# Reading index columns in place, with a memset ahead of each indirect transfer, in a graph network kernel

## What is computed

```python
h = relu(layernorm(x)); x = x + spmm(spmm(h))                 # L0: two weighted hops
h = relu(layernorm(x)); x = x + gcn(h, W, b)                   # L1: normalised by degree, one product
h = relu(layernorm(x)); x = x + (relu((h + sum_src h) @ W1.T + b1) @ W2.T + b2)        # L2
h = relu(layernorm(x)); x = x + update([h, sum_e message([h[src], h[dst], edge_attr])])  # L3: two small networks
```

## Time and profile before

| | us |
|---|---|
| median of 3 runs | 4911.03 |
| lowest, highest | 4899.02, 4911.47 |
| the profiled execution's own time | 4916.42 |
| its span, first to last instruction | 4914.2 |

### The profile page before, as it was taken

How to read it: one execution, slowest core, us unless ns; L and a number is a source line. 1 busy time by engine, 2 the same in 40 slices (tenths; PEclk the granted TensorE clock), 3 DMA queues, 4 the chain that set the end, 5 groups by cost and what they waited for, 6 DMA issues and landing times.

```text
span 4914.2 us, 62117 instructions
## 1 busy us (share of the span) xinstructions
PE 3612.6 (74%) x18706; PEld 2888.8 (59%) x18706; DVE 3039.2 (62%) x7232; ACT 2012.8 (41%) x5132; POOL 3807.9 (77%) x4405
## 2 busy tenths in 40 slices
PE   4767666666499999957777778878458787778784
PEld 2444344444399989945555556666346665656663
DVE  5634444444456566658888858888557666566661
ACT  3434434434311111135555555656225454454452
POOL 6788888888778888877788558888677888888875
PEclk8667767766655555578898989999779898998896
DMA  8433333332344454433343324444333223232220
GB/s 285 100 56 45 56 56 45 57 56 28 50 91 86 83 92 84 55 71 123 104 133 104 117 78 156 153 149 164 131 99 111 67 84 100 71 112 68 71 69 20
DMA packets 335499, 452.19 MB, mean 92 GB/s; under 512 B 208111, under 2 KB 233301, under 8 KB 334740
## 3 DMA queue, kind: packets, MB, share of 16 engines
q1 hardware_dynamic: 159268, 361.69, 20.9%
q0 software_dynamic: 176000, 87.72, 15.5%
HBM read 258.41 MB, written 225.53 MB: 98 GB/s over the span
## 4 chain that ended last, share of the span: by engine, by line
POOL 38%; issue 14%; PE 10%; DVE 6%; DMA 2%; ACT 2%; DVEq 0%; SPq 0%; POOLq 0%; ACTq 0%; another core or an unknown queue 0%
POOL ga L929 19%; POOL out_x L1062 8%; POOL isl L925 5%; POOL xu L1002 3%; PE tp L1259 2%; PE tp L1246 2%; POOL osl L925 2%; PE mm L1104 2%; PE mm L1123 1%; DMA xu<-acc,osl 1%; DVE xf L1948 1%; DVE wide L2107 1%; PE mm L1135 1%; PE mm L1097 1%; ACT zx L1597 1%
## 5 line engine op out<-in xcount | busy, mean ns | idle before, releaser
L929 POOL DMA_INDIRECT ga<-table,isl x784 | 838.8, 1070 | 224.4 <-issue 113.7
L1002 POOL DMA_INDIRECT xu<-acc,osl x392 | 625.1, 1595 | 144.8 <-issue 106.2
L1209 PE MATMUL tp<-xw,cc 128*128 128x394 f32 x784 | 411.5, 623 | 334.7 <-DVE cc L2015 243.3
L929 POOL DMA_INDIRECT ga<-xu,isl x392 | 424.1, 1082 | 111.8 <-POOL isl L925 61.5
L1062 POOL DMA_INDIRECT out_x<-acc,osl x392 | 418.6, 1068 | 114.5 <-POOL osl L925 80.8
L1209 PEld LDWEIGHTS tp<-xw,cc 128*128 128x128 f32 x784 | 141.3, 220 | 592.6 <-issue 324.9
L1246 PE MATMUL tp<-us,wide 128*128 128x64 f32 x1568 | 416.9, 422 | 88.9 <-DVE us L2143 50.0
L1246 PEld LDWEIGHTS tp<-us,wide 128*128 128x128 f32 x1568 | 379.9, 332 | 93.7 <-DVE us L2143 50.2
L1259 PE MATMUL tp<-acc,wide 128*128 128x64 f32 x1560 | 423.1, 427 | 0.8
L1194 PE MATMUL tp<-us,wide 128*128 128x64 f32 x1568 | 343.9, 421 | 69.6 <-DVE us L1932 60.8
L1562 ACT ACTIVATE acc<-tp,h 128x64 f32<-128x64 f32 x392 | 101.7, 310 | 693.2 <-PE tp L1259 541.9
(11 more groups left out here) (377 smaller groups left out, 9733.1 us busy)
## 6 DMA issues: line engine op xcount, KB each, us to landing
wide<-xu SPq DMA_DIRECT2D x84, 448.0 KB
zx<-key_rows SPq DMA_DIRECT2D x28, 896.0 KB
out_x<-wide SPq DMA_DIRECT2D x56, 448.0 KB
table<-acc SPq DMA_DIRECT2D x56, 448.0 KB
xf<-xs SPq DMA_DIRECT2D x56, 448.0 KB
wide<-table SPq DMA_DIRECT2D x56, 448.0 KB
xu<-in_x SPq DMA_DIRECT2D x25, 1000.0 KB
hop_even<-zeros SPq DMA_DIRECT2D x1, 12544.0 KB
```

Source lines behind the costliest of these rows:

```text
L929: nc.gpsimd.indirect_dma_start(o[:, g, :], None, table, bass.IndirectOffsetOnAxis(idx[:, g:g + 1], 0)).then_inc(s, 16)
L1002: nc.gpsimd.indirect_dma_start(xu, bass.IndirectOffsetOnAxis(osl[b][:, g:g + 1], 0), acc[b][:, g, :], None, compute_op=ALU.add).then_inc(f ...
L1209: f.key_row.raise_by(nc.tensor.matmul(tp[1][:, at:at + KEYS], reach[:, g * P:g * P + P], key_steps, start=True, stop=True), ("g", b, g))
```

## The change

POOL no longer copies index columns. The transfer is given the column of the big index tile itself. Ahead of each such transfer POOL now writes zeros to a tile `spacer` of 128 x 128 floats that nobody reads. The transfer does not wait for this memset; the next memset waits for the one before it. In `t_scatter` the wait for earlier scatters goes, since no slot is overwritten. All of it concerns the 56 gathers ahead of the first hop, the 392 + 392 gathers of the sparse stages, and the 784 transfers of the last stage: 1,624 in all. `hop0` and `hop1` stay as they are.

```diff
+        spacer = sb("spacer", [P, P])
...
-            def slot_copy(o, i_):
-
-                return nc.gpsimd.tensor_copy(o, i_).then_inc(s_slot, 1)
-
...
-            def gather_by_column(o, table, slot, index, c, s, copied):
+            def gather_spaced(o, table, index, c, s, spaced):
 
                 for g in range(G):
-                    slot_copy(slot[:, g:g + 1], index[:, c + g:c + g + 1])
-                    after.wait_ge(s_slot, copied + g + 1)
-                    gather(o, table, slot, s, (g,))
-                return copied + G
+                    if spaced + g:
+                        after.wait_ge(s_slot, spaced + g)
+                    nc.gpsimd.memset(spacer[:, :], 0.0).then_inc(s_slot, 1)
+                    gather(o, table, index[:, c:c + G], s, (g,))
+                return spaced + G
...
             for u in range(4):
-                copied = gather_by_column(ga_of[u], x, isl_of[u], dstc_i, u * G, f.got[u], copied)
+                spaced = gather_spaced(ga_of[u], x, dstc_i, u * G, f.got[u], spaced)
...
-                        copied = gather_by_column(ga[b], table, isl[b], index, ecol(i, b), f.got[b], copied)
-                    return copied
+                        spaced = gather_spaced(ga[b], table, index, ecol(i, b), f.got[b], spaced)
+                    return spaced
...
-            def t_scatter(i, copied, first=False):
+            def t_scatter(i, spaced):
                 for b in B2K:
                     after.wait_ge(*tt.o_ready.at(i, ("o", b)))
-                    if not first:
-
-                        after.wait_ge(tt.written[b], 16 * G * i)
                     for g in range(G):
-                        slot_copy(osl[b][:, g:g + 1], out_idx[:, tcol(i, b) + g:tcol(i, b) + g + 1])
-                        after.wait_ge(s_slot, copied + b * G + g + 1)
+                        after.wait_ge(s_slot, spaced + b * G + g)
+                        nc.gpsimd.memset(spacer[:, :], 0.0).then_inc(s_slot, 1)
                         nc.gpsimd.indirect_dma_start(
-                            out, bass.IndirectOffsetOnAxis(osl[b][:, g:g + 1], 0), acc[b][:, g, :], None,
+                            out, bass.IndirectOffsetOnAxis(out_idx[:, tcol(i, b) + g:tcol(i, b) + g + 1], 0),
+                            acc[b][:, g, :], None,
                             bounds_check=nodes_max, oob_is_err=False).then_inc(tt.written[b], 16)
-                return copied + 2 * G
+                return spaced + 2 * G
```

More of the change, by code:

```diff
@@ L380, in gnn @@
         s_answer = sem("prep_products_in_psum")
-        s_slot = sem("pool_slot_copied")
+        s_slot = sem("pool_spacer_written")
         s_turned = sem("keys_turned")
@@ L930, in gather @@
                         o[:, g, :], None, table, bass.IndirectOffsetOnAxis(idx[:, g:g + 1], 0)).then_inc(s, 16)
-            def gather_by_column(o, table, slot, index, c, s, copied):
+            def gather_spaced(o, table, index, c, s, spaced):
                 for g in range(G):
-                    slot_copy(slot[:, g:g + 1], index[:, c + g:c + g + 1])
-                    after.wait_ge(s_slot, copied + g + 1)
-                    gather(o, table, slot, s, (g,))
-                return copied + G
+                    if spaced + g:
[3 more added lines that the diff above has]
+                return spaced + G
             after.wait_ge(s_node, 1)
-            copied = 0
+            spaced = 0
             hop_max, all_max = pool.to_reg(ROWS + 4 * P - 1), pool.to_reg(ROWS + N + 4 * P - 1)
@@ L1019, in _, with body @@
                         after.wait_ge(sp_[0].kept[b], 2 * 16 * STEPS)
-                def body(i, first, copied):
+                def body(i, first, spaced):
                     for b in B2K if k == 0 else B2K[::-1]:
@@ L1028, in body @@
                                 after.wait_ge(*f.ga_free.at(i - 1, ("g", b)))
-                        copied = gather_by_column(ga[b], table, isl[b], index, ecol(i, b), f.got[b], copied)
-                    return copied
+                        spaced = gather_spaced(ga[b], table, index, ecol(i, b), f.got[b], spaced)
+                    return spaced
                 for i in range(STEPS):
-                    copied = body(i, i == 0, copied)
+                    spaced = body(i, i == 0, spaced)
                 for b in B2K:
@@ L1043, in _, with t_gather @@
                 after.wait_ge(s_fixed, 32 * (k + 1))
-            def t_gather(i, copied, first=False):
+            def t_gather(i, spaced, first=False):
                 for b in B2K:
@@ L1049, in t_gather @@
                         after.wait_ge(*tt.ga_free.at(i - 1, ("g", b)))
-                    copied = gather_by_column(ga[b], tables[1], isl[b], ptr_i, tcol(i, b), tt.got_a[b], copied)
-                return copied
-            def t_scatter(i, copied, first=False):
+                    spaced = gather_spaced(ga[b], tables[1], ptr_i, tcol(i, b), tt.got_a[b], spaced)
+                return spaced
+            def t_scatter(i, spaced):
                 for b in B2K:
                     after.wait_ge(*tt.o_ready.at(i, ("o", b)))
-                    if not first:
-                        after.wait_ge(tt.written[b], 16 * G * i)
@@ L1064, in t_scatter @@
                             bounds_check=nodes_max, oob_is_err=False).then_inc(tt.written[b], 16)
-                return copied + 2 * G
+                return spaced + 2 * G
             for q in LANES:
                 after.wait_ge(s_dense[q], 16 * DSTEPS)
[L1069 to L1073, removed]
+            spaced = t_gather(0, spaced, True)
@@ L1074, in _ @@
+            spaced = t_gather(1, spaced)
+            spaced = t_gather(2, spaced)
+            spaced = t_scatter(0, spaced)
+            spaced = t_gather(3, spaced)
             for i in range(2, STEPS - 2):
-                copied = t_scatter(i - 1, copied)
-                copied = t_gather(i + 2, copied)
+                spaced = t_scatter(i - 1, spaced)
+                spaced = t_gather(i + 2, spaced)
             for i in (STEPS - 3, STEPS - 2):
-                copied = t_scatter(i, copied)
+                spaced = t_scatter(i, spaced)
@@ L1083, in _ @@
                                          bounds_check=rows_max, oob_is_err=False).then_inc(s_head, 16)
-            t_scatter(STEPS - 1, copied)
+            t_scatter(STEPS - 1, spaced)
             after.wait_ge(s_border, 5)
```

## The result

The changed kernel takes 4707.15 us (median of 4 runs, 4706.33 to 4711.23), the kernel before 4907.63 us beside it: a ratio of 0.9595, with a 95% interval of 0.9579 to 0.9612. That is 4.05% or 200 us less. The forecast was 4726 us.

What follows compares the result with a forecast made beforehand. POOL, busy 77% of the span, was taken as the bound, with some 1263 transfers on the chain. Gaps 152 us plus stalls 53 less 20 given back left 185, so 4726 us; range 4630 to 4870.

Steps and rivals of the forecast that it cites:

- new gap 0.35 us, a gain of 0.12: POOL between indirect transfers: gap 0.01 + 0.14 + 0.20 = 0.35 us against 0.47; 1263 x 0.12 = 152 us.
- The memset's hold: Ahead of each transfer: 128 columns hold POOL 0.14 us, by a straight line between memsets of one and 448 columns.
- The stalls: POOL's copies beside VectorE instructions reading two full tiles: 107 us of stalls on the chain, half of them, 53 us, gained.
- What is given back: First sparse stage and last stage: 20 us taken off because VectorE and TensorE are close to binding.
- The larger gain: Rival, chance 0.20: transfer's start runs beside the memset, gap 0.30 us, no memset stalls; 282 us gained, 4629 us.
- My slower rival: Rival, chance 0.12: the 0.27 us ahead of a transfer is its own and stays; between 4927 and 4980 us.
- the smaller gain: Rival, chance 0.18: memset counts with 0.20 us and stalls like copies, or TensorE and VectorE bind at once; 4842 us.
- no effect: Rival, chance 0.05: waits for tiles take up the shorter round, or memset and stall cancel the gain; 4911 us.

## Why the prediction was right, point by point

The mechanism was right: the wait and the copies' stalls are what the change takes away, and both parts are seen by themselves. That the number is off by 19 us only is in part luck, since three terms were off and their errors nearly cancel.

**The wait.** Step "new gap 0.35 us, a gain of 0.12": measured 0.38 and 0.09, and 0.02 more from a gather that takes 0.95 instead of 0.97, which I hadn't foreseen. Idle ahead of a transfer came out at 0.16 to 0.17 us where I had 0.14. From start to start an undisturbed round of a gather fell by 0.108 us and that of a scatter by 0.084. Over the 1263 transfers on the chain (392 of them scatters) that makes an estimate of 127 us where the sum has 152. The 139 us of the run with the wait put back are another difference: the kernel with the waited memset has a gap of 0.49 us and not 0.47, since its memset is longer than the copy.

**The memset's hold.** A straight line through the memsets of the earlier trace rows was right in slope between 96 and 256 columns: the recorded medians are 0.192, 0.205, 0.219 and 0.327 us for 96, 112, 128 and 256, some 0.0009 us a column. The hold and the start together were put 0.03 us too short. For a single column the gap has a floor at 0.30 us, that of the earlier trace rows.

**The stalls.** I had 53 us, half of what copies lose. This was too small: the memsets lost next to nothing (median 0.219, mean 0.222 us ahead of gathers; 0.240 and 0.241 ahead of scatters), so nearly all of the 107 us went. Over all 1,624 rounds the copies took 438 us where undisturbed ones would have taken 313, the memsets 367 where 364 would do. That the run with waited memsets gives 59 us, close to my 53, is no proof of the half: it is what was left after POOL's longer waits for tiles. The rule of the Trainium skill (SBUF — State Buffer, Who interferes with whom), that VectorE's instructions with two inputs from SBUF hold up GpSimd's reads and not its writes, agrees with both sides now: 343 of the memsets ran beside a `TENSOR_TENSOR` of VectorE with two full inputs, and the longest of them took 0.256 us. A part of what they gained was lost elsewhere: scatters grew by 0.06 us each, 24 us over 392 of them, while their undisturbed time stayed near 0.98 us, so transfers did take over stalls there, as I had feared for all.

**What is given back.** This step was too small. In the first and the second sparse stage POOL's waits for VectorE rose from 13.6 and 40.0 us to 49.7 and 79.1, 75 us together, where I had taken off 20 (the 13.6 us stand in this row of the kernel before, the 40.0 in the earlier trace rows):

```profile
L925 POOL COPY isl<-map_idx 128x1 int32<-128x1 int32 x392 | 105.4, 269 | 18.1 <-DVE xc L2255 13.6 <-DMA xu<-hsum 1.2
```

Part of that is covered by counting only the 1263 transfers on the chain: over all 1,624 rounds POOL's own work got some 285 us shorter (100 us of busy time, 185 of idle time ahead of the transfers), and 210 of them reached the span. On the chain alone, 127 and 107 us less some 34 make the 200 that were measured; the sum had 152 and 53 less 20. By stage: 111 us in the last (forecast about 120), 51 in the second sparse stage (55 to 60, just missed), 45 in the first (20 to 40, missed), 4.5 ahead of them (5 at most).

**The rivals.** The larger gain (gap 0.30) can't be had with what was tried, and the reason is one that my prediction had nowhere: it took the memset for a mere cost. It costs POOL 0.08 us a round against bare transfers, and it is what makes the change a gain. Without it, or with one of 64 columns or less, the kernel is 18 to 20% slower than before. The changed kernel stands at 0.38 us, some 0.03 us from a loss of 800 us and more. My slower rival (the wait isn't what holds the transfer) fell at the idle time of 0.16 us, the smaller gain (memset counted in full and stalled) at the stalls, though its gap of 0.41 us was as near to 0.38 as my 0.35, and "no effect" at the time.

## What to carry to other kernels

A wait of one POOL instruction for another costs a tenth of a microsecond, and a copy there is stalled by VectorE where a memset isn't; over some 1,260 rounds on the path both are worth having. But gaps between indirect transfers are not to be closed as far as they will go: try the length of what stands between them from both sides (96 columns gave 0.9563, 0.9547 to 0.9579, against 0.9593, 0.9577 to 0.9609, for 112 beside it, and stand nearer to the cliff). Where the other engines get slower while POOL gets faster, look for waits on TensorE that have no named releaser.

## What the runs showed of the hardware that I had not expected

The last two columns are read from the semaphores' records: of the waits of ScalarE and VectorE that a TensorE semaphore ended (some 700 to 820 a run), how many ended over 1 us after the last TensorE instruction that raises it, and the longest such delay. TensorE's ends are modelled and some of its records can be missing, so a single delay can be off by more than the counts.

| between two transfers | gap, us | ratio to the kernel before | late | longest, us |
|---|---|---|---|---|
| nothing | 0.305 | 1.1847 | 193 | 46.8 |
| memset of 1 column | 0.305 | 1.1959 | 195 | 47.6 |
| memset of 64 | 0.329 | 1.1823 | 198 | 45.4 |
| copy of 1 | 0.355 | 1.1275 | 192 | 35.6 |
| memset of 96 | 0.358 | 0.9563 | 0 | |
| memset of 112 | 0.371 | 0.9593 | 0 | |
| memset of 128, the change | 0.384 | 0.9595 | 0 | |
| copy of 32 | 0.385 | 0.9783 | 0 | |
| memset of 256 ahead of every second | 0.490, 0.304 | 0.9610 | 0 | |
| copy of 1, waited for, to a slot (before) | 0.470 | 1 | 99 | 8.8 |
| copy of 128 | 0.471 | 1.0021 | 115 | 6.9 |
| copy of 1, waited for, index in place | 0.472 | 0.9992 | 103 | 7.6 |
| memset of 128, waited for | 0.491 | 0.9879 | 121 | 10.3 |
| memset of 256 | 0.492 | 0.9878 | 112 | 9.1 |

Long rows of indirect transfers with gaps of 0.355 us or less delay TensorE's signals to ScalarE and VectorE by tens of microseconds, at a DMA share of 0.12 to 0.33 in the two stretches shown, while signals from ScalarE arrive within 0.1 us. With gaps of 0.358 to 0.385 us this is gone. It isn't simply "the longer the better": with 0.47 us and more, the kernel before among them, about half as many signals are late again, by up to 10 us. They cost little there; the chain of the kernel before has 0% for "another core or an unknown queue", as the page calls unnamed releasers, that of the kernel with nothing between 11%:

```profile
POOL 38%; issue 14%; PE 10%; DVE 6%; DMA 2%; ACT 2%; DVEq 0%; SPq 0%; POOLq 0%; ACTq 0%; another core or an unknown queue 0%
...
another core or an unknown queue 11%; PE 9%; DVE 5%; issue 4%; ACT 2%; POOL 0%; DVEq 0%; POOLq 0%
```

Nor does a gap of 0.30 us do harm everywhere. In the two hops, where gathers and the longer adding scatters (1.58 us) have gaps of 0.30 us, none of the 240 to 270 such waits of a run ended over 1 us late, in any of these kernels. Why 0.36 to 0.385 us, or long and short gaps in turn, are free of it, and what the signals queue behind, wasn't found: neither the transfers' semaphore updates nor POOL's own handling was taken apart.
